# Reciprocals of the softmax sums: from VectorE to GpSimd, as a power of minus one

## The reference

```python
x = x + 0.5 * ffn(layernorm(x))      # 16 heads of 16, softmax attention, then two normed matmuls and a gelu
x = x + attn(layernorm(x))           # 8 heads, no softmax: linear attention, with biases
x = x + 0.5 * ffn(layernorm(x))
```

```python
q, k, v = heads(x @ Wq), heads(x @ Wk), heads(x @ Wv)      # 16 heads, depth 16
scores = einsum('bqd,bkd->bkq', q, k) / sqrt(256)
attn = softmax(scores, axis=-1)                            # over the queries
out = einsum('bkq,bkv->bqv', attn, v)
z = l2_normalize(out @ Wo); z = gelu(l2_normalize(z @ Wff))
```

## Time and profile before

| what | before |
|---|---|
| median of 3 runs | 2802.98 us (2802.79 to 2804.95) |
| the profiled execution | 2802.07 us, span 2800.2 us |
| PE busy | 2644.7 us (94%) |
| DVE busy | 2650.0 us (95%) |
| ACT busy | 2653.4 us (95%) |
| POOL busy | 1045.8 us (37%) |
| chain that ended last, by engine | PE 41%, ACT 37%, DVE 15%, issue 5%, POOL 1% |

### The profile page before, as it was taken

One profiled execution on the slowest core, in us unless ns is written; L12 is line 12 of the kernel. 1 busy time (PEld: TensorE's weight loads), 2 busy tenths in 40 slices (PEclk: granted clock), 3 DMA queues, 4 the chain that ended last, 5 costly groups with the idle time before them and its releaser, 6 DMA issues.

```text
span 2800.2 us, 87836 instructions
## 1 busy us (share of the span) xinstructions
PE 2644.7 (94%) x35680; PEld 1060.3 (38%) x35680; DVE 2650.0 (95%) x5349; ACT 2653.4 (95%) x4896; POOL 1045.8 (37%) x1662
## 2 busy tenths in 40 slices
PE   6899999999999999999999999999999999998986
PEld 2233443444443343433434333434334343332322
DVE  5999899998999999999999999999999999999995
ACT  4999999999999999999999999999999999999996
POOL 2325315353252432525325236153452615334222
PEclk9999999999999999999999999999999999999999
DMA  5331342323423244232443334444233443423230
GB/s 129 57 76 28 61 102 48 72 51 62 107 47 63 66 83 92 54 67 55 83 92 59 72 62 96 91 97 101 47 88 81 97 103 72 114 48 78 48 79 29
DMA packets 164869, 207.34 MB, mean 74 GB/s; under 512 B 34609, under 2 KB 97841, under 8 KB 164466
## 3 DMA queue, kind: packets, MB, share of 16 engines
q1 hardware_dynamic: 164082, 200.94, 34.1%
q0 software_dynamic: 384, 0.79, 0.2%
HBM read 43.39 MB, written 23.99 MB: 24 GB/s over the span
## 4 chain that ended last, share of the span: by engine, by line
PE 41%; ACT 37%; DVE 15%; issue 5%; POOL 1%; SPq 1%; DMA 0%; POOLq 0%; DVEq 0%
ACT exp_ring L927 33%; PE ring L1121 15%; DVE exp_ring L1010 13%; PE ring L1175 13%; PE o_acc L1186 11%; PE ring L1233 2%; ACT kq_stage L959 1%; ACT w_xn L938 1%; ACT ring L930 1%; ACT ring L933 1%; PE ring L1214 0%; DVE bn_stats L1060 0%; ACT L927 0%; ACT L938 0%; PE ring L1253 0%
## 5 line engine op out<-in xcount | busy, mean ns | idle before, releaser
L1010 DVE TENSOR_SCALAR_CACHE_REDUCE exp_ring<-ring 128x1024 f32<-128x1024 f32 x2048 | 2407.8, 1214 | 63.5 <-PE ring L1175 52.9
L927 ACT ACTIVATE exp_ring<-exp_ring,neg_max 128x1024 f32<-128x1024 f32 x2048 | 2329.2, 1146 | 62.6 <-DVE exp_ring L1010 59.2
L1175 PE MATMUL ring<-kq_stack 128*32 128x512 bf16 x16384 | 1193.2, 381 | 102.1 <-DVE exp_ring L1010 59.8
L1186 PE MATMUL o_acc<-exp_ring,v_scaled 128*32 128x512 f32 x8192 | 1052.0, 594 | 6.1 <-POOL v_scaled L865 4.9
L1175 PEld LDWEIGHTS ring<-kq_stack 128*32 128x32 bf16 x16384 | 402.8, 96 | 1077.1 <-DVE exp_ring L1010 419.1
L865 POOL TENSOR_TENSOR v_scaled<-v_now,exp_rsums 128x64 f32<-128x64 f32 x512 | 149.3, 293 | 1414.7 <-DVE exp_rsums L1020 1403.2
L927 ACT ACTIVATION_READ_ACCUMULATOR exp_ring<-exp_ring,neg_max 128x1 f32 x2048 | 399.5, 195 | 0.0
L1186 PEld LDWEIGHTS o_acc<-exp_ring,v_scaled 128*32 128x32 f32 x8192 | 250.4, 110 | 259.6 <-issue 61.0
L1121 PE MATMUL ring<-xn_T,ffn_wqkv 128*32 128x512 f32 x2048 | 257.8, 593 | 3.2 <-DVE exp_ring L1010 2.8
L1121 PE MATMUL ring<-ffn_wo_wowff,o_T 128*32 128x256 f32 x4096 | 243.0, 379 | 2.7 <-DVE exp_ring L1010 2.1
L1010 DVE DVE_READ_ACCUMULATOR exp_ring<-ring 128x1 f32 x2048 | 168.5, 82 | 0.0
(11 more groups left out here) (100 smaller groups left out, 1405.1 us busy)
## 6 DMA issues: line engine op xcount, KB each, us to landing
kq_stack<-kq_parts SPq DMA_DIRECT2D x2028, 64.0 KB, 2.4
x_slots<-x_post SPq DMA_DIRECT2D x13, 1024.0 KB, 4.8
x_post<-x_slots SPq DMA_DIRECT2D x13, 1024.0 KB, 6.9
x_post<-in_L_attn_x SPq DMA_DIRECT2D x8, 1024.0 KB, 9.0
x_prep<-x_slots SPq DMA_DIRECT2D x8, 1024.0 KB, 5.7
x_prep<-in_L_attn_x SPq DMA_DIRECT2D x7, 1024.0 KB, 7.8
out<-x_post SPq DMA_DIRECT2D x7, 1024.0 KB, 4.8
h_slots<-h SPq DMA_DIRECT2D x5, 256.0 KB, 2.1
```

What stands on the lines that cost most here:

```text
L927: nc.scalar.activation(e, e, ACT.Exp, bias=negmax[:, i % NM:i % NM + 1], scale=-1.0, accum_out=sums[:, g % EG, c:c + 1]).then_inc(exp_done, 1)
L1010: nc.vector.tensor_scalar(E[:, (g % EG) * HQ + c, :].rearrange("p (b n) -> p b n", b=NB), ps, -1.0, None, ALU.mult, ALU.min, accum_out=neg ...
L1175: last = mm(ps[k:k + COLS, n, :], kq[:, 0, c, j * P + k:j * P + k + COLS], kq[:, 1, c, n * BANK:(n + 1) * BANK], start=True, stop=True)
L1186: last = mm(O[32 * c:32 * c + 32, n, :], vsc[a][:, g % EG, c, :], E[:, (g % EG) * HQ + c, n * BANK:(n + 1) * BANK], start=(a == 0 and j == ...
```

## The change

DVE loses its 512 reciprocals. POOL computes them instead, as sum to the power of minus one, directly in front of each multiplication. A 128x4 tile of minus ones is filled once at the start. No entry of `TABLES` changes, so the power stands where the multiplication stood. POOL's wait for DVE's reciprocal becomes a wait for the group's last exp, and the multiplication now waits for POOL's own power.

```diff
+        minus_one = sb("minus_one", [P, HQ])
...
+            nc.gpsimd.memset(minus_one[:], -1.0).then_inc(const_ready, 1)
...
                 elif kind == "recip":
                     q, j = i // QG, i % QG
                     half, a = q // 2, q % 2
-                    pool.wait_ge(rsum_ready, nth("dve", "recip", p, i))
+                    pool.wait_ge(exp_done, nth("act", "tile", p, HQ * i + HQ - 1))
+                    nc.gpsimd.tensor_tensor(rsum[:, i % EG, :], sums[:, i % EG, :], minus_one[:], ALU.pow
+                                            ).then_inc(rsum_ready, 1)
+                    pool.wait_ge(rsum_ready, nth("pool", "recip", p, i))
...
-                elif kind == "recip":
-                    dve.wait_ge(exp_done, nth("act", "tile", p, HQ * i + HQ - 1))
-                    nc.vector.reciprocal(rsum[:, i % EG, :], sums[:, i % EG, :]).then_inc(rsum_ready, 1)
```

More of the change, by code:

```diff
@@ L808, in _ @@
             nc.gpsimd.memset(zero[:], 0.0).then_inc(const_ready, 1)
+            nc.gpsimd.memset(minus_one[:], -1.0).then_inc(const_ready, 1)
             nc.gpsimd.memset(ident[:], 0.0).then_inc(const_ready, 1)
-            pool.wait_ge(const_ready, 3)
+            pool.wait_ge(const_ready, 4)
             nc.gpsimd.affine_select(out=ident[:], in_=ident[:], compare_op=ALU.not_equal, fill=1.0,
@@ L814, in _ @@
                 nc.gpsimd.memset(vsc[a][:], 0.0).then_inc(const_ready, 1)
-            pool.wait_ge(const_ready, 6)
+            pool.wait_ge(const_ready, 7)
             for (kind, p, i), _ in ORDER["pool"]:
@@ L991, in _ @@
                 if kind == "setup":
-                    dve.wait_ge(const_ready, 6)
+                    dve.wait_ge(const_ready, 7)
                     nc.vector.tensor_reduce(mask[:], ident[:].rearrange("p (k j) -> p j k", j=AH),
@@ L1122, in mm_cols @@
                 return last
-            pe.wait_ge(const_ready, 6)
+            pe.wait_ge(const_ready, 7)
             pe.wait_ge(wqkv_loaded, 3 * 16)
```

## The result

The changed kernel takes 2869.39 us in the median of 4 runs (2867.43 to 2870.48), the kernel before 2802.89: the ratio is 1.0232, with a 95% interval of 1.0219 to 1.0244. It is 66.5 us slower. I had forecast 2832 us with a range from 2804 to 2857. The direction was right; the +30 us that I forecast are less than half of what came. The profiled execution took 2868.55 us, with a span of 2866.8.

What follows compares the result with a forecast made beforehand. The bound was read by phase: PE in 2, PE, ACT and DVE shared in 6, ACT's exps on 11's chain, DVE in 0. Terms 16.5 + 15 + 0 − 2.5 + 1 = +30 us on 2802.07 gave 2832, range 2804 to 2857.

Steps and rivals of the forecast that it cites:

- The prices: Per group on POOL: power 1.02 us, hand-over 0.1; POOL busy near 1570 us; phase 0 gains 2.5 us.
- The first burst of phases 1 to 3: POOL's packed run mid-phase makes PE 6.6 us late; 5.5 us lost a phase, 16.5 for three.
- one burst a phase: The forecast's count: each phase priced at one packed run of POOL, by its longest delay.
- phases 14, 15 and the tail: DVE's relief against one or two small waits, and the last group's power before the last `av`: +1 us.
- phases 4 to 8's first burst: POOL's packed run makes PE 4.1 us late; 3.0 us a phase taken, 15 for five.
- Phases 9 to 13: PE 1.5 us late once a phase against up to 2.9 us of DVE relief; sum taken as 0.
- The 573 us: Extra time on POOL from all 512 powers, of which 522 us busy.
- DVE's total less by some 46 us: Sign expected in the changed profile: 512 reciprocals removed at 0.09 us of DVE's time each.
- DVE's relief wins: Rival: POOL's bursts absorb the powers, phases 0 and 9 to 13 give back 17 us, 2785 us; chance 0.10.
- The delays add up: Rival: POOL's late results delay PE, DVE and ACT in turn, phases 1 to 8 lose twice, 2863 us; chance 0.08.

Runs made afterwards that it cites:

- h2: Changed kernel's powers on POOL only for groups 16 to 31 of each phase, DVE's reciprocals as before elsewhere: 2832.93 us, ratio 1.0104 to the kernel before.
- h1: Changed kernel's powers on POOL only for groups 0 to 15 of each phase, DVE's reciprocals as before elsewhere: 2840.64 us, ratio 1.0134 to the kernel before.
- e1: Changed kernel without the power, POOL multiplying v by the sums, so neither engine computes a reciprocal: 2797.77 us, ratio 0.9986 to the kernel before.
- b1: Kernel before with only the tile of minus ones filled and the counts raised, DVE's reciprocals kept: 2805.20 us, ratio 1.0008.
- e5: Changed kernel with a power over one column (128x1), the first head's reciprocal scaling all four heads: 2827.48 us, ratio 1.0087 to the kernel before.
- e4: Changed kernel with a multiplication by minus one in place of the power, same waits and hand-over: 2805.47 us, ratio 1.0013 to the kernel before.
- e2: Kernel before, DVE's reciprocals in use, plus an unread spare 128x4 power on POOL ahead of each multiplication: 2886.47 us, ratio 1.0297.
- h3: POOL's powers only for groups 0 to 2, 14 to 16 and 26 to 31 of each phase, DVE's reciprocals elsewhere: 2803.64 us, ratio 1.0006.

## Why the prediction was wrong

**The prices were right.** The power takes 1.01 us (I took 1.02), the multiplication starts 0.08 us behind it (0.1), and POOL is busy 1563 us (near 1570). DVE gave back 2.9 us in phase 0 (2.5).

**The first burst of phases 1 to 3 was right.** I had the multiplication that ended at 275.36 us late by 7.3, so at 282.7. POOL's and PE's timelines of the changed kernel, in phase 1:

```profile
280.98 1.05 POOL L863 TENSOR_TENSOR exp_rsums<-exp_sums,minus_one 128x4 f32<-128x4 f32 x1
282.10 0.30 POOL L870 TENSOR_TENSOR v_scaled<-v_now,exp_rsums 128x64 f32<-128x64 f32 x1
```

```profile
269.74 1.41 PE L1188 MATMUL o_acc<-exp_ring,v_scaled 128*32 128x512 f32 x8 [2.79 <-POOL v_scaled L870]
...
282.45 1.07 PE L1188 MATMUL o_acc<-exp_ring,v_scaled 128*32 128x512 f32 x8 [1.04 <-POOL v_scaled L870]
```

It ends at 282.40, and its `av` starts at 282.45 instead of 276.06, 6.4 us late (I had 6.6). PE pays in pieces (2.79 us at one group, 1.04 at this one). By the middle of the phase DVE's reductions stand 6.0 us behind those of before; I had taken 5.5.

**The step that failed: one burst a phase.** The prediction priced one place in each phase and no other: the first packed run in phases 1 to 8, and in phases 9 to 13 the second one (the multiplication at 1905.11 is that of group 23). But phases 1 to 8 have a second one too, phase 14 has one, and each costs by itself. In the changed kernel PE waits for the multiplication in the second half of a phase above all at groups 20 and 22 in phases 1 to 3, 18 and 19 in 4 to 8, 22 and 23 in 9 to 13, and 21 in phase 14. In phases 4 to 8 the run follows when the DMAs of the last stack have read `kq_parts`: POOL then makes two splits and the multiplications between and behind them without a stop. POOL's timeline of the changed kernel in phase 6, then PE's (groups 18 and 19):

```profile
1246.95 0.62 POOL L690 TENSOR_SCALAR kq_parts<-kq_stage 128x512 bf16<-128x512 f32 x1 [9.68 <-DMA kq_stack<-kq_parts]
...
1250.87 1.01 POOL L863 TENSOR_TENSOR exp_rsums<-exp_sums,minus_one 128x4 f32<-128x4 f32 x1
1251.95 0.29 POOL L870 TENSOR_TENSOR v_scaled<-v_now,exp_rsums 128x64 f32<-128x64 f32 x1
...
1256.12 1.01 POOL L863 TENSOR_TENSOR exp_rsums<-exp_sums,minus_one 128x4 f32<-128x4 f32 x1
1257.21 0.29 POOL L870 TENSOR_TENSOR v_scaled<-v_now,exp_rsums 128x64 f32<-128x64 f32 x1
```

```profile
1252.30 1.07 PE L1188 MATMUL o_acc<-exp_ring,v_scaled 128*32 128x512 f32 x8 [0.98 <-POOL v_scaled L870]
1257.56 1.06 PE L1188 MATMUL o_acc<-exp_ring,v_scaled 128*32 128x512 f32 x8 [2.04 <-POOL v_scaled L870]
```

In front of that run POOL is idle for 9.68 us, so a mean over the half phase shows nothing. Phase 14 has the same pattern, and there PE waits 2.81 us at one group:

```profile
2633.13 1.93 PE L1188 MATMUL o_acc<-exp_ring,v_scaled 128*32 128x512 f32 x8 [2.81 <-POOL v_scaled L870]
```

These matmuls take 1.93 us and not 1.06, at a granted clock of 0.50, so here the wait does bring a second cost. In h2 the low stretch at this place is twice as long, and the phase loses 4.5 us instead of 2.8.

h2 shows that these second halves cost without the first: +27 us in its profile, +31 in the median, with phases 9 to 13 and the start in it. In the changed kernel, by the step of DVE's reductions, second bursts cost about 1.1 us in each of phases 1 to 3, 13 us over phases 4 to 8 (35.2 less the 22 that were lost by the middle), and 3 in phase 14. That makes 19 us. The prediction had 1 for phases 14, 15 and the tail together and none for the others, so this step is some 18 of the 36.5 us.

**The term that was too small: phases 4 to 8's first burst.** I worked out 4.1 us and took 3.0, "behind it the three engines have 1.4 to 3.3 us of slack". The lateness on PE was well worked out. The `av` that was to be 4.1 us late started at 992.17 − 916.5 = 75.7 us of phase 5 before. Now that phase begins at 942.6:

```profile
1022.81 1.06 PE L1188 MATMUL o_acc<-exp_ring,v_scaled 128*32 128x512 f32 x8 [0.61 <-POOL v_scaled L870]
```

This is at 80.2 us of the phase, 4.5 us late. (PE had already waited 1.62 us four groups earlier, where I had priced nothing.) By DVE's reductions the changed kernel stands 3.1 us behind by the middle of phase 4 and 4.6 to 4.9 in the others; of the difference, phase 4 of the kernel before had lost 1.7 to the clock itself. h1, where the rest of the phase is untouched, lost 3.0 to 4.9 over the whole phase. So nothing was made up in the second half: the 1.4 to 3.3 us that each of the three engines stood idle there weren't slack that PE could use. What should have been 22 us for the five phases I took as 15: about 7 of the 36.5 us.

**Phases 9 to 13.** I balanced 1.5 us of wait against DVE's relief and took 0. The wait is there (+1.2 a phase), the relief isn't: e1 finds these phases no shorter, though DVE is busy 99% in phase 11. The chain had said so the earlier trace rows, and I should have followed it: 6 of the 36.5 us.

**The start.** 2.8 us that I hadn't thought of; b1 ties 1.8 of them to the fill of a tile.

**Small slips.** The 573 us that the powers should bring POOL come from 1.12 us a group; with the 1.1 that the bursts are worked out with they are 563, and 1.09 was measured (558). "DVE's total less by some 46 us" didn't come either: it was 20.

**The rivals.** "DVE's relief wins" put break-even at 0.8 us a group; e5 lost 25 us at 0.63. The rule of the Trainium skill, GPSIMD Engine Reference, "Performance versus the Vector engine", which has GpSimd at half of VectorE's speed, led to 2788 us there. That ratio was measured on an add of 2048 columns. It doesn't carry over to the pair here, which isn't even the same instruction on both engines: a power of four columns takes POOL 1.01 us, a reciprocal takes DVE 0.17. With e4's product of four columns, 0.20 us on POOL, an exchange would have been nearly even. "The delays add up" came nearest in time (2863), by a mechanism that the profile doesn't show: PE's waits for `x_prep` and `w_xn` are 6.5 us in all and DVE's for x1 11.0, beside 66.7 for `v_scaled` at the matmuls alone and 107.0 at their weight loads.

**What stays open.** Why 17 us, and not 4, lie between e2 and the changed kernel is explained by the time at which the power can begin, and argued only. And why a fill of 16 bytes a partition delays the first tiles isn't known: in b1 and in the changed kernel PE waits longer for the first stacks' DMAs, with the same instructions ahead of them.

## What to carry to other kernels

Before an operation goes to an engine that is busy a third of the time, look at that engine's timeline and mark every stretch where it doesn't stop, two or three in each phase and not the worst one. In such a stretch the price is the count of moved instructions times their duration, minus the idle time on the way, and here nothing of it came back, since the engines around it were full. And take the worth of the relief from the chain of waits: DVE was busy 95%, and taking 512 instructions from it was worth 4 us.

## What the hardware showed that I had not expected

- POOL's power costs by the column: 0.55 us for 128x1, 1.01 for 128x4 and 1.65 for 128x8 (before, L820), 0.15 to 0.16 us a column on top of 0.4. Its product of 128x4 takes 0.20 us.
- A reciprocal of 171 ns on DVE is nearly hidden: removing 512 of them (e1) lowered DVE's busy time by 24 us, 0.05 us each, and the time by 4.
- A low clock costs PE nothing where it waits for a late engine anyway (phases 1 and 3 against 2), and 1.5 to 1.7 us at two other places (phase 4 before, the start of phase 1 in h2 and h3).
- A fill of a 128x4 tile at the start goes with a first reduction at 40.3 us instead of 38.5 and 38.6, in one profile of it and two without.
